# Second attention's scores as two float32r passes over stacked rows, with the splits on GpSimd and the operands held once

## The reference

```python
q = (xw @ wq + bq).reshape(-1, T, NH, HD)
k = (xw @ wk + bk).reshape(-1, T, NH, HD)
logits = jnp.einsum('nthd,nThd->nhtT', q, k) / np.float32(np.sqrt(HD))
bias_h = jnp.einsum('nabhd,akd->nhabk', qg, Rh)
bias_w = jnp.einsum('nabhd,bkd->nhabk', qg, Rw)
logits = logits + bias_h[..., :, None] + bias_w[..., None, :]
attn = jax.nn.softmax(logits, axis=-1)
out = jnp.einsum('nhtT,nThd->nthd', attn, v).reshape(-1, T, NH * HD)
```

## Time and profile before

| What | Value |
|---|---|
| Time, median of 3 runs | 911.3 us |
| The 3 runs | 907.35, 911.3, 1135.42 us |
| Profiled execution: span from the first to the last instruction | 916.1 us |
| PE busy | 810.4 us (88%) |
| PE weight loads busy | 681.9 us (74%) |
| DVE busy | 517.0 us (56%) |
| ACT busy | 434.8 us (47%) |
| POOL busy | 130.5 us (14%) |

### The profile page before, as it was taken

How to read it: one execution, slowest core, us unless ns; L and a number is a source line. 1 busy time by engine, 2 the same in 40 slices (tenths; PEclk the granted TensorE clock), 3 DMA queues, 4 the chain that set the end, 5 groups by cost and what they waited for, 6 DMA issues and landing times.

```text
span 916.1 us, 20164 instructions
## 1 busy us (share of the span) xinstructions
PE 810.4 (88%) x6794; PEld 681.9 (74%) x6794; DVE 517.0 (56%) x1517; ACT 434.8 (47%) x1419; POOL 130.5 (14%) x239
## 2 busy tenths in 40 slices
PE   3349498999899998879997999999999999997998
PEld 2338377777676777569996788887888888876998
DVE  7016365666567666834542666656575757574442
ACT  1005354455455555534433555656465655555432
POOL 7000011011101101003232010101010110100211
PEclk9558788989899999968999899999999999999999
DMA  4237201001010100000004030403122130400001
GB/s 119 49 72 171 40 5 31 15 20 23 12 26 7 33 18 18 2 1 1 1 1 70 1 71 2 71 6 66 29 42 47 22 67 3 70 1 1 19 18 35
DMA packets 39535, 29.85 MB, mean 33 GB/s; under 512 B 12429, under 2 KB 37793, under 8 KB 39457
## 3 DMA queue, kind: packets, MB, share of 16 engines
q1 hardware_dynamic: 38433, 27.29, 15.2%
q0 software_dynamic: 1024, 1.57, 0.9%
HBM read 8.79 MB, written 1.57 MB: 11 GB/s over the span
## 4 chain that ended last, share of the span: by engine, by line
PE 65%; SPq 19%; DVE 7%; issue 4%; DMA 3%; ACT 1%; POOL 1%; DVEq 0%; POOLq 0%; ACTq 0%
PE bank L1187 9%; SPq L1118 8%; PE bank L1266 8%; PE bank L482 7%; PE bank L461 7%; PE bank L1214 5%; PE bank L891 4%; PE bank L1194 4%; PE bank L1233 3%; SPq L1111 3%; SPq L1533 3%; PE bank L1326 3%; PE bank L908 3%; PE bank L1009 2%; SPq L1543 2%
## 5 line engine op out<-in xcount | busy, mean ns | idle before, releaser
L651 ACT ACTIVATE Pb<-bank,nmax 128x256 f32<-128x256 f32 (+1 forms) x432 | 192.3, 452 | 126.0 <-DVE nmax L641 118.8
L641 DVE TENSOR_REDUCE nmax<-bank 128x2 f32<-128x392 f32 (+2 forms) x240 | 138.8, 578 | 41.4 <-PE bank L1187 29.4
L662 DVE TENSOR_SCALAR Pb<-Pb,rsum 128x196 f32<-128x196 f32 (+2 forms) x432 | 132.9, 345 | 8.5
L891 PE MATMUL bank<-K,Q 96*128 96x196 f32 x384 | 94.1, 373 | 33.3 <-DMA Q<-dense_k 32.8
L681 ACT COPY area<-bank 98x392 f32<-98x392 f32 (+1 forms) x144 | 77.1, 536 | 95.2 <-PE bank L1194 68.7
L1187 PE MATMUL bank<-K,Q 96*128 96x256 f32 x384 | 105.2, 399 | 6.3 <-DMA Q<-rel_dense 6.1
L891 PEld LDWEIGHTS bank<-K,Q 96*128 96x128 f32 x384 | 71.5, 217 | 37.8 <-issue 30.3
L1187 PEld LDWEIGHTS bank<-K,Q 96*128 96x128 f32 x384 | 68.0, 194 | 26.1 <-issue 15.6
L651 ACT ACTIVATION_READ_ACCUMULATOR Pb<-bank,nmax 128x1 f32 x432 | 87.3, 202 | 0.0
L681 DVE COPY area<-bank 60x128 f32<-60x128 f32 (+2 forms) x96 | 43.4, 452 | 71.2 <-PE bank L908 29.6
L471 ACT ACTIVATE area<-bank,fc1b 128x256 f32<-128x256 f32 x96 | 45.0, 474 | 70.1 <-PE bank L461 69.7
(11 more groups left out here) (137 smaller groups left out, 1494.1 us busy)
## 6 DMA issues: line engine op xcount, KB each, us to landing
Q<-dense_q SPq DMA_DIRECT2D x16, 288.0 KB, 4.9
K<-dense_k SPq DMA_DIRECT2D x16, 288.0 KB, 7.0
Q<-dense_q SPq DMA_DIRECT2D x48, 32.0 KB, 2.0
K<-dense_k SPq DMA_DIRECT2D x48, 32.0 KB, 2.0
Q<-rel_dense SPq DMA_DIRECT2D x32, 48.0 KB, 3.2
Q<-rel_dense POOLq DMA_DIRECT2D x32, 48.0 KB, 2.9
out<-x_all SPq DMA_DIRECT2D x8, 192.0 KB, 2.0
x_all<-in_x SPq DMA_DIRECT2D x1, 1344.0 KB, 7.7
```

The costliest lines, as they stand in the source:

```text
L641: nc.vector.tensor_reduce(nmax[0:sc.shape[0], u % 3, 0:sc.shape[1]], sc, AX.X, ALU.max, negate=True).then_inc(self.m_rdy, 1)
L651: nc.scalar.activation(Pb[u % 3][0:rows, t, 0:cols], sc[:, t, :], ACT.Exp, bias=nmax[0:rows, u % 3, t:t + 1], accum_out=esum[0:rows, u % 3 ...
L662: nc.vector.tensor_scalar(Pb[u % 3][0:rows, t, 0:keep], Pb[u % 3][0:rows, t, 0:keep], rsum[0:rows, u % 3, t:t + 1], None, ALU.mult).then_i ...
L891: mm = nc.tensor.matmul(S_BANK[u % 3][:, t * N0:(t + 1) * N0], Q0[p][:, h, t * P:(t + 1) * P], k, start=True, stop=True)
```

## The change

In float32r a product takes one pass where float32 takes more, but rounds its operands. The change splits q, k and the relative terms into a high part (rounded to float32r) and a low part (the rest), and writes the score product as q_high k_high + q_low k_high + q_high k_low, plus the relative terms high and low times the constant pattern. The terms are stacked along the contraction, so that two matmuls give the sum: pass A of 128 rows (q_high on k_high, q_low on k_high again, the relative terms' high part on the pattern) and pass B of 80 rows (q_high on k_low, the relative terms' low part on the pattern), accumulated in PSUM.

- The splits: for each of the six head pairs POOL does a copy and a subtract for q and for k (24 operations on 96x256), and for the relative terms three copies and three subtracts (128x256). k_low and rel_low lie where dense_k and rel_dense lay.
- The scatters: Q1 and K1 no longer alternate by image but hold pass A ([0]) and pass B ([1]), once. Each image's scatter is in two halves of 6 heads. A half may be overwritten once the previous image's scores of those 6 heads are done (`operands_free`). A half has 12 DMAs of 144 KB for q and k and 4 of 48 KB for the height terms on SP, and 4 of 48 KB for the width terms on POOL. Heads are ordered so that three heads of a DMA lie side by side.
- The fronts of a1 move one slot ahead (`X_SLOT` = 1, `V_SLOT` = 6), and the statistics of the next image come at the start of slot 0.
- The constant pattern is loaded once into hot1 with the `later` loads and copied to K1[0] and K1[1] when m0 begins; the two loads of it in `late` and `late_odd` go.

```diff
             def emit_scores(self, eng, n, u):
-                p = n.parity
-                if u == 0:
-                    eng.wait_ge(self.scat, n.at(64, 64))
-                    eng.wait_ge(self.relscat, n.at(64, 64))
-                    eng.wait_ge(self.relscat_w, n.at(64, 64))
+                if u % HG == 0:
+                    eng.wait_ge(self.scat[u // HG], n.at(192, 192))
+                    for kind in range(2):
+                        eng.wait_ge(self.relscat[kind][u // HG], n.at(64, 64))
+                h = self.slot_of(u)
                 for t in range(NT):
-                    mm = nc.tensor.matmul(S_BANK[u % 3][:, t * T:(t + 1) * T], Q1[p][:, u, t * P:(t + 1) * P],
-                                          K1[p][:, u, :], start=True, stop=True)
+                    q = slice(t * P, (t + 1) * P)
+                    nc.tensor.matmul(S_BANK[u % 3][:, t * T:(t + 1) * T], Q1[0][:, h, q], K1[0][:, h, :],
+                                     start=True, stop=False)
+                    mm = nc.tensor.matmul(S_BANK[u % 3][:, t * T:(t + 1) * T], Q1[1][0:K1BROWS, h, q],
+                                          K1[1][0:K1BROWS, h, :], start=False, stop=True)
...
             def sp(self, eng):
                 def image(n):
...
+                    for half in range(2):
+                        self.operands_free(eng, n, half)
                         land(eng, "sp")
+                        eng.wait_ge(self.q_split, n.at(2 * NPAIR, HG * half + HG))
+                        land(eng, "sp")
+                        eng.wait_ge(self.k_split, n.at(2 * NPAIR, HG * half + HG))
+                        land(eng, "sp")
+                        self.scatter_qk(eng, half)
+                        eng.wait_ge(self.rel_split, n.at(6, 6))
+                        land(eng, "sp")
+                        self.scatter_rel(eng, half)
...
             def pool_front(self, eng, n):
...
+                for half in range(2):
+                    if n.counts(192, 0):
+                        eng.wait_ge(self.scat[half], n.at(192, 0))
+                    for g in range(3 * half, 3 * half + 3):
+                        eng.wait_ge(self.g_out[0], n.at(11, 2 + g))
+                        land(eng, "pool")
+                        nc.gpsimd.tensor_copy(q_high[:, g, :], self.qd[:, g, :]).then_inc(self.q_split, 1)
+                        eng.wait_ge(self.q_split, n.at(2 * NPAIR, 2 * g + 1))
+                        nc.gpsimd.tensor_tensor(q_low[:, g, :], self.qd[:, g, :], q_high[:, g, :].bitcast(F32),
+                                                ALU.subtract).then_inc(self.q_split, 1)
...
+                self.rel_scattered(eng, n)
                 for b in range(2):
                     eng.wait_ge(self.g_out[b], n.at(11, 9))
                 land(eng, "pool")
-                self.scatter_rel(eng, n, (2, 3))
+                for g in range(3):
+                    nc.gpsimd.tensor_copy(rel_high[:, g, :], rel_dense[:, g, :]).then_inc(self.rel_split, 1)
+                    eng.wait_ge(self.rel_split, n.at(6, 2 * g + 1))
+                    nc.gpsimd.tensor_tensor(rel_low[:, g, :], rel_dense[:, g, :], rel_high[:, g, :].bitcast(F32),
+                                            ALU.subtract).then_inc(self.rel_split, 1)
+                eng.wait_ge(self.rel_split, n.at(6, 6))
+                for half in range(2):
+                    self.operands_free(eng, n, half)
+                    land(eng, "pool")
+                    self.scatter_rel(eng, half, 1)
...
         def constant_rows(i):
-            return [(K1[i][D0:K0ROWS], per_head(a["c_hot0"])), (K1[i][K1REL:K1ROWS], per_head(a["c_hot1"])),
+            return [(K0[i][D0:K0ROWS], per_head(a["c_hot0"])),
```

More of the change, by code:

```diff
@@ L62 @@
 K1ROWS = K1REL + 2 * H
+K1AREL = 2 * D1
+K1BREL = D1
+K1BROWS = K1BREL + 2 * H
+HG = HEADS // 2
 NEG = -1.0e30
@@ L317, in build @@
                  (fc2b[0][:], bcast(a["L0_conv_fc2_b"])), (fc2b[1][:], bcast(a["L1_conv_b2"]))]
+        later += [(hot1[:], a["c_hot1"])]
         later += norm_loads(1, "L0_conv_norm2_w", "L0_conv_norm2_b")
@@ L781, in step @@
                     for u in range(self.NU):
+                        if which == "dve" and u == 0 and has_next and self.X_SLOT == 1:
+                            self.dve_stats(eng, n.next())
                         slot(eng, n, u, has_prev, ahead)
@@ L788, in step @@
                             for f in fronts.get(u, ()):
[L789 removed]
+                                if f not in (self.pe_transpose_x, self.dve_xhat, self.act_xn) \
+                                        and not (f == self.dve_stats and self.X_SLOT == 1):
                                     f(eng, n.next())
@@ L813, in pe_slot @@
                 self.pe_probsT(eng, n, u)
-                if u == 2 and ahead(self.NU - 1, 1):
+                if u == self.X_SLOT and ahead(self.NU - 1, 1):
                     self.pe_transpose_x(eng, n.next())
@@ L839, in dve_slot @@
                     self.dve_ao(eng, m, g)
-                if u == 1 and ahead(self.NU - 1, 1):
+                if u == self.X_SLOT - 1 and ahead(self.NU - 1, 1):
                     self.dve_xhat(eng, n.next())
@@ new lines, in rel_scattered, with scatter_rel @@
+            def rel_scattered(self, eng, n):
+                if n.counts(64, 0):
+                    for kind in range(2):
+                        for half in range(2):
+                            eng.wait_ge(self.relscat[kind][half], n.at(64, 0))
+            def scatter_rel(self, eng, half, kind=0):
+                for dst, row, src in ((Q1[0], K1AREL, rel_high), (Q1[1], K1BREL, rel_low)):
+                    for j in range(2):
+                        at, lines = HG * half + 3 * j, 64 * kind + 32 * half + H * j
+                        eng.dma_start(dst[row + H * kind:row + H * (kind + 1), at:at + 3, :].bitcast(F32),
+                                      src[lines:lines + H, :, :].bitcast(F32))\
+                           .then_inc(self.relscat[kind][half], 16)
@@ L1414, in setup @@
                 self.qd, self.kd, self.reld = dense[0][:], dense[1][:], rel_dense[:]
-                self.relscat_w = sem("a1_relscat_w")
+                self.scat = [sem("a1_scatter0"), sem("a1_scatter1")]
+                self.relscat = [[sem(f"a1_relscat{kind}{half}") for half in range(2)] for kind in "hw"]
+                self.q_split = sem("a1_q_split")
+                self.k_split = sem("a1_k_split")
+                self.rel_split = sem("a1_rel_split")
                 self.x_whole = [sem("a1_x0"), sem("a1_x1")]
@@ L1546, in _ @@
             stage_start(sp, 1)
+            sp.wait_ge(ld_later, 16 * len(later))
+            for dst, row in ((K1[0], K1AREL), (K1[1], K1BREL)):
+                sp.dma_start(dst[row:row + 2 * H].bitcast(F32), per_head(hot1[:])).then_inc(hot1_done, 16)
             a1.sp(sp)
```

122 lines of the change are left out of this document (62 added, 60 removed).

## The result

The change makes the kernel a little slower. Its median is 918.6 us (913.3 to 929.2, 20 runs) against 913.9 us for the kernel before on the same chip; the ratio is 1.0055, 95% interval [1.0035, 1.0075]. The forecast was 890 us, with 872 to 920 as its range: the time lies inside the range, but I had called the change faster, and it is not. The profiled execution went from a span of 916.1 us to 920.8.

A forecast was written before the change was run, and what follows sets the result against it. PE's own stream was taken to bound a1. Seven images -19.6, last image -1.5, a1's start +3.5, a0's startup -4: -21.6 us, from 911.3 to 890, range 872 to 920.

The forecast's parts named there:

- The score passes: PE's scores per head: two float32r passes take 0.57 us instead of 0.92, saving 0.35 per head, 4.2 per image.
- The rival that a pass over 128 rows would save nothing: PE's scores: a 128-row float32r pass costs half a float32 product, POOL's work hides, 911 us; chance 0.06.
- POOL's durations: POOL's splits at 256 elements: copies 0.41 us, subtracts 0.73, with waits 1.2 per copy and subtract.
- the slower rival: POOL's serial splits end last; at 0.3 us more per operation slot 9 waits 8.2, 944 us; chance 0.12.
- The chain to slot 9: From slot 2's start through relative products, copies, POOL's splits, issue and landing: operands there at 27.7 us, wanted at 27.0.
- time lost to VectorE: POOL's splits before slot 9: 1.5 us added because VectorE holds the shared port pair.
- their copies end about 1 later: Relative terms' copies out of PSUM end about 1 us after PE ends the relative products at 17.1.
- The stall: PE's wait in slot 9 for the scattered operands: 1.0 us per image, bounds 0 and 9.
- The layer norm moved ahead: DVE brings x out of PSUM before slot 2's first projection: 2.3 us against PE's 2.0, charged 0.3 (0 to 0.4).
- VectorE: 0.5 us charged: DVE's normalising multiplies wait for POOL's instructions: 4 us of DVE per image, 0.5 charged to the period, bounds 0 and 3.
- the rival of VectorE as the bound: Nine of twelve multiply pairs pay 1.09 us, DVE sets the pace in slots 5 to 0, 902 us; chance 0.20.
- The period: Time per image of a1: PE's stream 38.6 plus 1.0, 0.5 and 0.3 makes 40.4 us, 2.8 less than before.

## Why the prediction was wrong

**The score passes: right.** 0.57 us a head was forecast, 0.48 to 0.61 measured. The rival that a pass over 128 rows would save nothing is out. With no splits at all the kernel reaches 883 us, 31 us below the kernel before by the ratio, the moved layer norm and the moved loads included.

**POOL's durations: right.** Copies take 0.39 to 0.46 us and subtracts 0.73 to 0.74, as the interpolation gave. The price at which I let the slower rival decide, 0.8 us an operation, was never reached, and yet the slower side came true. I had made its condition a question of durations, and it was one of the length of the chain.

**The chain to slot 9: mis-sized in two terms.** From slot 2's start at 598.61 to the operands the prediction had 27.7 us, the trace has 628.30 - 598.61 = 29.7. Term by term:

```
term                                        forecast   measured
PE ends the relative products               17.1       18.4
their copies out of PSUM, to POOL's start   1.0        2.9
six splits                                  3.6        3.6
time lost to VectorE                        1.5        0
to the operands' landing                    4.5        4.8
```

The step that failed is "their copies end about 1 later". It was the one duration in that sum with no row behind it, and two rows on record had it: the products ended at 619.44 and POOL issued at 623.98, 4.5 us later, with no split between. ScalarE's timeline before shows why:

```profile
621.04 0.59 ACT L681 COPY area<-bank 128x512 f32<-128x512 f32 x1 [3.79 <-PE bank L1194]
622.07 0.37 ACT L1222 COPY area<-bank 128x256 f32<-128x256 f32 x1 [0.44 <-PE bank L1214]
622.34 0.97 ACT L1345 COPY rel_dense<-bank 64x384 f32<-64x384 f32 x2
```

The copies wait in order behind PT's copy and the value product's, and end at 623.3, 3.9 us behind the products. I took 1.0 for all of it. It takes 2.9 in the changed kernel, where no value product's copy stands in front; these 1.9 us more are as much as PE's whole wait. Of the 1.3 us more on PE, 0.5 is the wait for x (3.7 us in 7) and 0.2 one for k's copies (1.7 in 7); the rest wasn't followed up. These waits hold PE up on its way to slot 9 too: it was ready at 628.30 - 1.90 - 598.61 = 27.8, not 27.0. So the wait is 29.7 - 27.8 = 1.9 where the sum had 27.7 - 27.0 = 0.7. What I added for VectorE's hold nearly hid both errors: without it the forecast wait would have been zero and the error plain.

**The stall: 2.0 us against 1.0, and its echo left out.** I charged the wait and nothing for what follows it. The clock fell behind six of seven waits and took 1.5 to 1.7 us of each of those images, nearly as much as the wait itself. This is the second step that failed, a term put at nothing, and the largest single one in the period. The two belong together: with the copies' 1.0 true, there would have been next to no wait for the clock to fall behind. Before, the same wait was 0.4 us and the stretches stayed at full clock, so no row showed it; but the bounds of the stall (0 to 9) had no clock in them either.

**The layer norm moved ahead: 0.5 to 1.1 us against 0.3** (bounds 0 to 0.4). I had counted only the way of x out of PSUM in slot 1. The waits for P and for xhat in slots 0 and 1, where DVE has the statistics, the normalising and the maximum at once, were not in it.

**VectorE: 0.5 us charged.** The idle operations on GpSimd cost the kernel before nothing; the q and k splits cost the changed one 0.5 us an image (40.2 against 39.7), about half of it a wait of PE for k's copies (1.8 us in 7) that is not there without splits. The term was right in size, and the rival of VectorE as the bound refuted.

**The period, then.** What was forecast as 38.6 + 1.0 + 0.5 + 0.3 = 40.4 is 38.5 (before's mean of 42.7 less 4.2) + 0.5 + 1.1 + 2.0 + 1.4 = 43.5, against 43.6 measured; the last term is the clock's 1.7 in five of six periods. The pieces agree with most runs: no splits 39.7, no relative splits 40.2, everything 43.6, and with the relative terms split out of PSUM and without the move 39.1. They don't agree with one: no splits and no move should give 38.5, and its undisturbed periods are 39.3 to 39.6. So the 1.1 may be too much, and up to 0.6 us of the period then has no cause shown.

**The ends: smaller than forecast, and in part not to be told from scatter.** To a1's first scores the start of a1 took +1.8 against +3.5 (bounds 2 to 12); the +3.3 in the table owes the rest to the period in it. Ahead of a1 it is -5.6 against -4, but only the 2 to 3 us of the moved loads are shown: the kernel with idle operations on GpSimd, whose code up to a1 is that of before, came to a1's first q projection at 476.4, and the kernel before at 481.8. So the term came near by luck. The last image gave +0.5 instead of -1.5. The second MLP's +1.2 is no work of the change either: it takes 81.4 us in that same kernel and 79.5 in the one without relative splits, against 79.8 before and 81.0 after.

## What to carry to other kernels

When an operation is put into a chain that ends just in time, read the whole chain of before from its first to its last instruction in the timeline, queueing included, and add to that; don't rebuild it from durations. An engine that is idle 70% of the time can still be the wrong place for six short operations, and an instruction that sits in order behind an unrelated copy costs as much as a slow one. Where a new wait on TensorE comes back each turn, price what the clock does behind it as well, and look first for a place where the split falls out of a copy that is made anyway.

## What the runs showed of the hardware

- TensorE waited some 2 us at a time. Behind these waits the granted clock was 0.57 to 0.61 for 4 us in six of seven images, and 1.00 in one. Eight matmuls of the value product took 1.08 us at 619.09, ahead of a wait, and 1.98 at 586.58, behind one.
- VectorE and GpSimd side by side cost VectorE far less than the pair of rows suggested: 47 ns a multiply on average beside idle operations and 21 in the changed kernel, not 0.7 us a pair. On the whole image it was 1.1 and 0.5 us where I had taken 4. The Trainium skill's exclusive lock ("SBUF — State Buffer", section "SBUF: two separate sides") isn't refuted by this: in the changed kernel's trace, between 510 and 840 us, 67 of the 186 multiplies lie beside a split or xbias on GpSimd and take 0.51 us on average, at most 0.90; the other 119 take 0.35. Before, the seven beside the one of 1.01 us took 1.44.
- ScalarE wrote the high part out of PSUM as float32r in 0.47 us for 64x384, VectorE the difference in 0.56 (mean of 28 each): the same as the plain copies they replace (0.55 for VectorE's in the kernel before).
- DMAs between parts of SBUF moved 210 to 250 GB/s in the stretches behind slot 9, where the earlier trace rows had 188.
